# Two attentions and six layer normalisations of a decoder on one core: the softmax in row tiles, the normalisation as a pipeline over turns

## The chip, the cores and the metric

The kernel runs on one NeuronCore of one Trainium2 chip. The metric is the device time of one execution in microseconds (us), taken as the median of several executions. TensorE (PE in the profile) multiplies and transposes, VectorE (DVE), ScalarE (ACT) and GpSimd (POOL) do the rest, SyncE (SP) issues the transfers. Each engine works through its own queue in order and waits on semaphores that others raise.

## What is computed

Two decoder layers over x of 8 batches x 256 tokens x 256 features, in float32. Every sublayer is x = x + f(layernorm(x)):

```python
# layer 0: attn (causal, 16 query heads, 4 key/value heads, width 128), xattn over 64 sets, 16 experts
# layer 1: a gated delta rule (16 key heads, 32 value heads), cross attention, 48 experts
def _layernorm(x, axis=-1, eps=1e-05):
    m = jnp.mean(x, axis=axis, keepdims=True); v = jnp.var(x, axis=axis, keepdims=True)
    return (x - m) / jnp.sqrt(v + eps)
# L0 attention
scores = jnp.einsum('bkgqd,bksd->bkgqs', qg, k) * scale        # rope on q, k
attn = jax.nn.softmax(scores + causal, axis=-1)
out = jnp.einsum('bkgqs,bksd->bkgqd', attn, v)
# L1 cross attention: keys and values from 64 context rows and the 256 own rows,
# q and k first divided by their root mean square, then rope, softmax over 320 keys
```

## The kernel before, in words

The program is six blocks, one after another, with a barrier of all engines between them: self attention, set attention, routed experts, delta attention, cross attention, sparse experts. Each begins with a call of `layernorm` (L155), six in all.

**layernorm** goes over the 16 tiles of 128 tokens in four turns of four tiles. In a turn VectorE takes the statistics of four tiles (L181, L184), adds epsilon (L186); GpSimd raises to the power -1/2 (L200); VectorE scales the four tiles (L191); TensorE transposes their eight halves into banks 0 and 1 of `k.ps[0]` (L213); ScalarE copies the 128x1024 result to `xnT` (L223). VectorE has one set of statistics tiles, so turn i+1's statistics start only behind turn i's scaling, and it waits for GpSimd in each turn.

**attention** (L271) serves both attentions; `cross` tells them apart. The work is 16 units for each of two halves h (a key/value head with its G=4 query heads and one batch of 256 tokens, TB=2 row tiles). `schedule` (L346) gives every engine the same list of stages: in stage(h, front, back) the half h projects and rotates its new unit (front), while the other half g does scores, softmax, mixing and the output projection of its unit (back). Of 33 stages 31 have both; most run inside a hardware loop. The four query heads r of the back unit are done in two pairs, 0 and 1 in the first half of the stage, 2 and 3 in the second.

The queues within a stage, which set the order around the change:

- TensorE (L477): score 0, 1; project_q (L405, in cross attention one of its two tiles stands before the scores); turn_probs 0, 1 (L455); mix 0, 1 (L465); score 2, 3 (L441); project_kv (L413); turn_probs 2, 3; mix 2, 3; turn_qk (L425, L428) and give (L473), give first in cross attention.
- VectorE (L620): row_max 0, 1 (L583, L589), norm_probs 0, 1 (reciprocal L597, scaling L600), keep_probs 0, 1 (L609, L611), rotate of the two query tiles (L535 to L537), row_max 2, 3, norm_probs 2, rotate of keys, norm_probs 3, keep_probs 2, 3, in cross attention rms (L563 to L566), add_halves (L553), rms_keys (L571, L575), add_out (L617).
- ScalarE (L696): exps 0, 1 (L679), keep_probs 0, 1 (L686, L689), keep_mix 0, 1 (L694), exps 2, 3, keep_probs 2, then keep_v (L661 to L666; it waits for `rotated`, raised by the rotation of the keys), keep_probs 3, keep_mix 2, 3, keep_qk (L670, L671).
- GpSimd: the power of the sums of squares (L379, cross attention alone), the copies of tokens (L371, L373).

A semaphore of a head counts once for both row tiles: `scored`, `max_ready`, `exp_done`, `probs_ready`. mix of head r waits for both parts of keep_probs(r), ScalarE's and VectorE's.

## Time and profile before

| | us |
|---|---|
| median of 3 runs | 4150.28 (4146.95 to 4150.4) |
| the profiled execution | 4138.86 |
| its span | 4137.1 |
| TensorE busy | 3579.5, 87% |
| VectorE busy | 2639.7, 64% |
| ScalarE busy | 1644.6, 40% |
| GpSimd busy | 1412.7, 34% |

Self attention fills about 26 to 675 us of the span, cross attention about 2944 to 3870 us, delta attention about 1150 to 2889 us. The busy shares are means over blocks with different limits, so the stages of the two attentions are to be read one instruction at a time. The clock in the profile is the granted TensorE clock, 1.00 for 2.4 GHz and 0.50 for 1.2 GHz. The profiled execution is 11.4 us (0.3%) shorter than the median of the runs.

### The profile page before, as it was taken

The numbers are of one execution on the slowest core, as the hardware profiler recorded it, in microseconds if no ns is written. First come the engines' busy times: TensorE is split into PE (matmuls) and PEld (weight loads), VectorE is DVE, ScalarE is ACT, GpSimd is POOL, SyncE is SP. The second block draws the span as 40 slices with busy tenths as digits, with TensorE's granted clock in tenths as the row PEclk, the third lists the DMA queues.
The fourth block names the chain that finished last, engine by engine and source line by source line (L and its number), as shares of the span: only waits on it lengthen the run. The fifth ranks groups of instructions, "written<-read, shape, count | busy, mean of one in ns | idle before, by whom it ended". The sixth has DMA issues, their size and how long they took to land. (4 is left out here: it accounts for less than half of the span.)

```text
span 4137.1 us, 57933 instructions
## 1 busy us (share of the span) xinstructions
PE 3579.5 (87%) x17616; PEld 2756.4 (67%) x17616; DVE 2639.7 (64%) x7558; ACT 1644.6 (40%) x4218; POOL 1412.7 (34%) x2085
## 2 busy tenths in 40 slices
PE   7999997589678999999999999998499999999565
PEld 5676765445366888888888888886356556556454
DVE  5666565532247888888888888873666666666531
ACT  3444442133234455555554545441243443443221
POOL 0000000068615555555555555552111111111055
PEclk9999998589868999999999999999699999999665
DMA  2000002335500111111111111110100000000346
GB/s 75 0 0 0 0 0 68 116 65 85 117 14 19 40 28 40 29 36 30 35 37 27 37 27 39 28 21 12 57 1 0 0 0 0 0 0 0 115 111 144
DMA packets 220951, 149.99 MB, mean 36 GB/s; under 512 B 117104, under 2 KB 208656, under 8 KB 220208
## 3 DMA queue, kind: packets, MB, share of 16 engines
q1 hardware_dynamic: 193664, 111.49, 10.5%
q0 software_dynamic: 22848, 31.69, 4.6%
q10 hardware_dynamic: 4224, 4.19, 0.3%
q8 instruction: 104, 1.70, 0.2%
q14 instruction: 111, 0.91, 0.1%
HBM read 105.64 MB, written 41.61 MB: 36 GB/s over the span
## 5 line engine op out<-in xcount | busy, mean ns | idle before, releaser
L1921 DVE SCALAR_TENSOR_TENSOR dl_y<-ps,dl_taps,dl_y 128x255 f32<-128x255 f32 (+2 forms) x1536 | 652.4, 474 | 129.5 <-ACT dl_y L1817 125.3
L1652 PE MATMUL ps<-xnT,dl_wkqv 128*128 128x256 f32 x2048 | 546.2, 393 | 27.5 <-DVE dl_lp L1964 21.8
L1652 PEld LDWEIGHTS ps<-xnT,dl_wkqv 128*128 128x128 f32 x2048 | 370.7, 194 | 78.3 <-issue 34.9
L379 POOL TENSOR_TENSOR at_rs<-at_ss,mhalf 128x15 f32<-128x15 f32 x32 | 125.5, 3922 | 745.1 <-DVE at_ss L566 745.1
L1575 POOL TENSOR_TENSOR dl_rn<-dl_n,mhalf 128x4 f32<-128x4 f32 x128 | 173.4, 1354 | 548.0 <-DVE dl_n L1937 548.0
L465 PE MATMUL ps<-at_shared,at_v 128*128 128x256 f32 (+2 forms) x1280 | 315.7, 380 | 4.6
L1817 ACT ACTIVATE dl_y<-ps,dl_taps 128x256 f32<-128x256 f32 x512 | 260.2, 560 | 106.1 <-PE ps L1652 106.0
L405 PE MATMUL ps<-at_wq,at_xb 128*128 (+1 forms) x512 | 247.6, 618 | 36.0 <-POOL at_xb L373 33.9
L441 PE MATMUL ps<-at_kT,at_qT 128*128 128x320 f32 (+2 forms) x1024 | 271.2, 397 | 2.8 <-ACT at_kT L671 2.8
L1593 POOL TENSOR_TENSOR dl_inv_u<-dl_inv_u,dl_inv_tmp 64x30 f32<-64x30 f32 (+14 forms) x480 | 260.1, 542 | 37.6
L465 PEld LDWEIGHTS ps<-at_shared,at_v 128*128 128x128 f32 (+1 forms) x1280 | 211.1, 190 | 89.3 <-issue 64.0
L455 PE MATMUL ps<-ident,at_probs 128*128 128x128 f32 (+1 forms) x1152 | 173.8, 283 | 96.2 <-DVE at_probs L600 93.0
L473 PE MATMUL ps<-at_wo,at_oT 128*128 (+1 forms) x1024 | 234.8, 382 | 18.7 <-ACT at_oT L694 18.7
L1677 PE MATMUL ps<-dl_wo,dl_z 128*128 128x256 f32 x1024 | 245.9, 384 | 1.3 <-issue 1.3
L1590 POOL TENSOR_TENSOR dl_inv_tmp<-dl_inv_u,dl_inv_a 64x30 f32<-64x30 f32 (+14 forms) x480 | 233.5, 486 | 24.7
L455 PEld LDWEIGHTS ps<-ident,at_probs 128*128 128x128 f32 (+1 forms) x1152 | 124.1, 135 | 169.2 <-DVE at_probs L600 156.1
L1825 ACT ACTIVATE dl_z<-dl_y 128x512 f32<-128x512 f32 x256 | 161.6, 631 | 180.9 <-DVE dl_y L1921 180.9
L371 POOL COPY at_xb<-xnT 128x512 f32 (+1 forms) x64 | 39.1, 612 | 567.6 <-PE ps L413 562.8
L1663 PE MATMUL ps<-dl_z 128*128 128x512 f32 (+1 forms) x512 | 227.6, 528 | 0.0
L473 PEld LDWEIGHTS ps<-at_wo,at_oT 128*128 128x128 f32 x1024 | 189.4, 190 | 54.7 <-issue 27.5
L441 PEld LDWEIGHTS ps<-at_kT,at_qT 128*128 128x128 f32 x1024 | 175.3, 191 | 70.4 <-ACT at_kT L671 13.5
L583 DVE TENSOR_REDUCE at_mx<-ps 128x2 f32<-128x640 f32 x128 | 105.5, 825 | 180.5 <-PE ps L441 176.9
(348 smaller groups left out, 7798.5 us busy)
## 6 DMA issues: line engine op xcount, KB each, us to landing
dl_grow<-decay_rows SPq DMA_DIRECT2D x128, 128.0 KB, 3.0
sp_wgu<-in_w1gu SPq DMA_DIRECT2D x12, 768.0 KB, 5.3
dl_wkqv<-in_w1kqv SPq DMA_DIRECT2D x16, 512.0 KB, 4.6
delta_diag<-dl_lp SPq DMA_DIRECT2D x512, 8.0 KB
dl_diag<-delta_diag_tt SPq DMA_DIRECT2D x512, 8.0 KB, 1.7
moe_wgu<-in_w0gu SPq DMA_DIRECT2D x16, 448.0 KB, 10.6
sp_wd<-in_w1d SPq DMA_DIRECT2D x12, 384.0 KB, 6.2
dl_wo<-in_w1o SPq DMA_DIRECT2D x16, 256.0 KB, 3.6
```

The lines of the kernel that those rows point to most:

```text
L405: last = nc.tensor.matmul(k.ps[h][:, t, :], xb[h][:, c, t * P:(t + 1) * P], wq[:, c, ds(group(u) * (G * HD), G * HD)], start=c == 0, stop= ...
L441: last = nc.tensor.matmul(o[:, 0:nk], qT[h][:, r, t * P:(t + 1) * P], kT[h][:, 0:nk], start=True, stop=cross)
L455: last = nc.tensor.transpose(slot(h, (r % 2) * 4 + pieces[j])[0:w, t * P:(t + 1) * P], probs[h][:, (r % 2) * TB + t, j * P:j * P + w], k.i ...
L465: last = nc.tensor.matmul(slot(h, (r % 2) * 4 + 3)[:, c0:S], v[h][0:w, j, :], pT[h][0:w, r % 2, j, c0:S], start=j == 0, stop=j == KT - 1)
L473: last = nc.tensor.matmul(slot(h, t), oT[h][:, hh, t * P:(t + 1) * P], wo[:, ds(group(u) * G + hh, 1), :], start=hh == 0, stop=hh == G - 1)
L1590: nc.gpsimd.tensor_tensor(tmp, inv_u[:, 0:i, i:i + 1].to_broadcast([GP, i, w]), inv_a[:, i:i + 1, i + 1:Q32].to_broadcast([GP, i, w]), ALU ...
L1593: nc.gpsimd.tensor_tensor(inv_u[:, 0:i, i + 1:Q32], inv_u[:, 0:i, i + 1:Q32], tmp, ALU.subtract)\
L1652: last = nc.tensor.matmul(bank(h, m // 2, (m % 2) * S, (m % 2 + 1) * S), wkqv[h][:, c, m * P:(m + 1) * P], k.xnT[:, c, u.seq * S:(u.seq + ...
L1663: last = nc.tensor.matmul(bank(h, blk, 0, 2 * (S - blk * P)).rearrange("p (a s) -> p a s", a=2), z[h][:, 0, blk * P:(blk + 1) * P], z[h][: ...
L1677: last = nc.tensor.matmul(bank(h, 3, t * D, (t + 1) * D), z[h][:, 2 + m, t * P:(t + 1) * P], wo[h][:, m, :], start=m == 0, stop=m == 1)
L1817: last = nc.scalar.activation(y[h][:, m, :], bank(h, m // 2, (m % 2) * S, (m % 2 + 1) * S), ACT.Identity, bias=taps[h][:, m, KC:KC + 1], s ...
L1921: last = nc.vector.scalar_tensor_tensor(y[h][:, m, back:S], bank(h, m // 2, (m % 2) * S, (m % 2 + 1) * S - back), taps[h][:, m, KC - 1 - b ...
```

## The change

1. `layernorm` keeps two sets of statistics tiles. VectorE takes turn i+1's statistics before it scales turn i. It scales two of the four tiles; ScalarE scales the other two with an Identity activation whose scale is the inverse deviation and whose bias is minus mean times it, which VectorE computes in one small instruction (`ln_nmr`). Turns alternate between banks 0, 1 and 2, 3, and ScalarE's copy of turn i comes behind its scaling of turn i+1.
2. The softmax of both attentions goes by row tile: the four semaphores count each tile. The VectorE order of a pair of heads is max r t0, max r t1, max r+1 t0, norm r t0, max r+1 t1, norm r t1, norm r+1 t0, keep_probs r, norm r+1 t1, in the function `softmax`.
3. The rotation of the keys stands behind the whole `softmax` of heads 2 and 3 instead of between their scalings.
4. GpSimd's power is split into one element of the context keys and the 10 columns of the two token tiles (before: 15 columns at once, with a memset of ones ahead of the loop, now gone).

```diff
@@ layernorm, VectorE
-            for i in range(turns):
+            def stats(i):
...
+                if n >= 2:
+                    dve.wait_ge(k.ln_normed_d, n - 1)
...
+            def normalise(i):
+                n, b = i + base, i % 2
+                if n >= 1:
+                    dve.wait_ge(k.ln_normed_a, n)
+                    dve.wait_ge(k.ln_turned_d, n)
+                dve.wait_ge(k.ln_pow, n + 1)
+                nc.vector.scalar_tensor_tensor(k.ln_nmr[b][:, HQ:Q], k.ln_mv[b][:, HQ:Q, 0], -1.0, k.ln_rstd[b][:, HQ:Q],
+                                               ALU.mult, ALU.mult).then_inc(k.ln_shift, 1)
+                for q in range(HQ):
...
+            stats(0)
+            for i in range(turns):
+                if i + 1 < turns:
+                    stats(i + 1)
+                normalise(i)
@@ layernorm, TensorE (and the same for the other two tiles behind ln_normed_a)
+                n, b = i + base, 2 * (i % 2)
+                if n >= 2:
+                    pe.wait_ge(k.ln_stored, n - 1)
+                pe.wait_ge(k.ln_normed_d, n + 1)
@@ layernorm, ScalarE
             for i in range(turns):
-                act.wait_ge(k.ln_turned, i + base + 2)
-                nc.scalar.copy(k.xnT[:, :, i * Q * P:(i + 1) * Q * P], k.ps[0][:, 0:DC, :]).then_inc(k.ln_stored, 1)
+                n, b = i + base, i % 2
+                if n >= 1:
+                    act.wait_ge(k.ln_turned_a, n)
...
+                act.wait_ge(k.ln_shift, n + 1)
+                for q in range(HQ, Q):
+                    last = nc.scalar.activation(xn(i, q), k.x[:, i * Q + q, :], ACT.Identity,
+                                                bias=k.ln_nmr[b][:, q:q + 1], scale=k.ln_rstd[b][:, q:q + 1])
+                last.then_inc(k.ln_normed_a, 1)
+                if i >= 1:
+                    keep(i - 1)
+            keep(turns - 1)
@@ attention, GpSimd
-                    nc.gpsimd.tensor_tensor(rs[h][:, :, :], ss[h][:, :, :],
-                                            k.mhalf[:, 0:KT * (G + 1)].rearrange("p (t g) -> p t g", t=KT), ALU.pow)\
+                    nc.gpsimd.tensor_tensor(rs[h][0:CTX, TB, G:G + 1], ss[h][0:CTX, TB, G:G + 1], k.mhalf[0:CTX, 0:1], ALU.pow)
+                    nc.gpsimd.tensor_tensor(rs[h][:, 0:TB, :], ss[h][:, 0:TB, :],
+                                            k.mhalf[:, 0:TB * (G + 1)].rearrange("p (t g) -> p t g", t=TB), ALU.pow)\
                         .then_inc(s.rms_ready[h], 1)
@@ attention, TensorE: score raises scored once a tile; turn_probs
-                    pe.wait_ge(s.probs_ready[h], u * G + (r + 1))
+                    pe.wait_ge(s.probs_ready[h], u * (G * TB) + (r * TB + 1))
+                    for j in range(2 if cross else 1):
+                        turn(j, 0)
+                    pe.wait_ge(s.probs_ready[h], u * (G * TB) + (r * TB + 2))
+                    for j in range(2):
+                        last = turn(j, 1)
+                    if cross:
                         for t in range(TB):
+                            last = turn(2, t)
@@ attention, VectorE
+                def softmax(h, u, r):
+                    row_max(h, u, r, 0)
+                    row_max(h, u, r, 1)
+                    row_max(h, u, r + 1, 0)
+                    norm_probs(h, u, r, 0)
+                    row_max(h, u, r + 1, 1)
+                    norm_probs(h, u, r, 1)
+                    norm_probs(h, u, r + 1, 0)
+                    keep_probs(h, u, r)
+                    norm_probs(h, u, r + 1, 1)
@@ stage, VectorE
                     if back is not None:
-                        row_max(g, back, 0)
-                        row_max(g, back, 1)
-                        norm_probs(g, back, 0)
-                        norm_probs(g, back, 1)
-                        keep_probs(g, back, 0)
+                        softmax(g, back, 0)
                         keep_probs(g, back, 1)
                     if front is not None:
                         rotate(h, front, 0)
                         rotate(h, front, 1)
                     if back is not None:
-                        row_max(g, back, 2)
-                        row_max(g, back, 3)
-                        norm_probs(g, back, 2)
+                        softmax(g, back, 2)
                     if front is not None:
                         rotate(h, front, TB)
                     if back is not None:
-                        norm_probs(g, back, 3)
-                        keep_probs(g, back, 2)
                         keep_probs(g, back, 3)
@@ exps, ScalarE
-                    act.wait_ge(s.max_ready[h], u * G + (r + 1))
                     for t in range(TB):
+                        act.wait_ge(s.max_ready[h], u * (G * TB) + (r * TB + t + 1))
...
-                    last.then_inc(s.exp_done[h], 1)
+                        last.then_inc(s.exp_done[h], 1)
```

row_max(h, u, r, t) is one reduction of one tile (128, 256 or 320 columns), a wait for it, and the small instruction that forms the exp's bias; norm_probs(h, u, r, t) is one reciprocal, a wait for it, and one scaling.

## Rows read from the trace of the kernel before

**Rows 1.** Busy time by stretch (PE, PEld, DVE, ACT, POOL, clock, DMA): self and cross attention.
```profile
300.00:400.00 100.00, 92.16 (x480) 69.90 (x478) 61.54 (x196) 40.03 (x135) 3.08 (x5) 1.00 0.00 0
...
3300.00:3400.00 100.00, 92.12 (x399) 61.02 (x400) 60.79 (x162) 40.62 (x106) 17.43 (x12) 1.00 0.00 0
```
**Rows 2.** Timeline of TensorE, self attention: start, length, line, idle before it and releaser.
```profile
313.13 0.55 PE L455 MATMUL ps<-ident,at_probs 128*128 128x128 f32 x3 [0.92 <-DVE at_probs L600]
...
315.46 1.09 PE L425 MATMUL ps<-ident,at_t 128*128 128x128 f32 x8 [0.40 <-DVE at_t L553]
```
**Rows 3.** Timeline of VectorE in the same stage.
```profile
304.21 0.55 DVE L600 TENSOR_SCALAR at_probs<-at_probs,at_rden 128x128 f32<-128x128 f32 x2
306.01 0.62 DVE L611 COPY at_shared<-ps 128x128 f32<-128x128 f32 x2 [1.26 <-PE ps L455]
306.55 0.68 DVE L535 TENSOR_TENSOR at_t<-ps,rope_cos 128x512 f32<-128x512 f32 x1
...
309.07 0.61 DVE L589 TENSOR_REDUCE at_mx<-ps 128x1 f32<-128x128 f32 x2
...
309.82 0.62 DVE L589 TENSOR_REDUCE at_mx<-ps 128x1 f32<-128x128 f32 x2
...
310.87 0.17 DVE L597 RECIPROCAL at_rden<-at_den 128x2 f32<-128x2 f32 x1 [0.22 <-ACT at_probs L679]
...
313.72 0.29 DVE L611 COPY at_shared<-ps 128x128 f32<-128x128 f32 x1 [0.44 <-PE ps L455]
313.92 1.48 DVE L553 TENSOR_TENSOR at_t<-at_t 128x1280 f32<-128x1280 f32 x1
```
**Rows 4.** Timeline of TensorE, one cross-attention stage.
```profile
3312.88 0.87 PE L455 MATMUL ps<-ident,at_probs 128*128 128x128 f32 x6 [0.26 <-DVE at_probs L600]
3313.59 3.34 PE L465 MATMUL ps<-at_shared,at_v 128*128 128x256 f32 x12
...
3323.55 0.87 PE L455 MATMUL ps<-ident,at_probs 128*128 128x128 f32 x6 [1.10 <-DVE at_probs L600]
```
**Rows 5.** Timeline of VectorE in the same stage.
```profile
3312.74 0.41 DVE L609 COPY at_shared<-ps 64x256 f32<-64x256 f32 x1
...
3318.24 0.82 DVE L583 TENSOR_REDUCE at_mx<-ps 128x2 f32<-128x640 f32 x1 [1.52 <-PE ps L441]
...
3322.50 0.21 DVE L537 TENSOR_TENSOR at_t<-ps,rope_sc 64x64 f32<-64x64 f32 x1
```
**Rows 6.** Timeline of ScalarE in the same stage.
```profile
3322.97 1.03 ACT L661 ACTIVATE at_shared<-ps 128x1024 f32<-128x1024 f32 x1
...
3324.72 0.61 ACT L686 COPY at_shared<-ps 128x512 f32<-128x512 f32 x1
...
3327.64 0.37 ACT L694 COPY at_oT<-ps 128x256 f32<-128x256 f32 x1 [1.31 <-PE ps L465]
```
**Rows 7.** Timeline of all engines, second layernorm: first turn and last copy.
```profile
676.19 1.41 DVE L181 BATCH_NORM_STATS2 ln_stats<-x 128x6 f32<-128x256 f32 x4 [0.89 <-PEq L99]
...
679.42 1.38 DVE L191 TENSOR_SCALAR ln_xn<-x,ln_mv,ln_rstd 128x256 f32<-128x256 f32 x4 [1.20 <-POOL ln_rstd L200]
...
680.86 1.97 PE L213 MATMUL ps<-ident,ln_xn 128*128 128x128 f32 x8 [6.28 <-DVE ln_xn L191]
...
696.38 1.01 ACT L223 COPY xnT<-ps 128x1024 f32<-128x1024 f32 x1 [3.49 <-PE ps L213]
```
**Rows 8.** Busy time by stretch, columns as in rows 1, end of the first layernorm.
```profile
24.00:26.00 2.00, 1.09 (x6) 0.69 (x4) 0.00 (x0) 0.87 (x1) 0.00 (x0) 1.00 0.00 0
```
**Rows 9.** Timeline of TensorE: the first projection of self attention.
```profile
27.20 6.33 PE L405 MATMUL ps<-at_wq,at_xb 128*128 128x512 f32 x8 [2.10 <-POOL at_xb L371]
```
**Rows 10.** Groups by line and shape: count | busy us, mean ns | idle before.
```profile
L600 DVE TENSOR_SCALAR at_probs<-at_probs,at_rden 128x320 f32<-128x320 f32 x256 | 87.3, 383 | 4.5
...
L379 POOL TENSOR_TENSOR at_rs<-at_ss,mhalf 128x15 f32<-128x15 f32 x32 | 125.5, 3922 | 745.1 <-DVE at_ss L566 745.1
...
L1817 ACT ACTIVATE dl_y<-ps,dl_taps 128x256 f32<-128x256 f32 x512 | 260.2, 560 | 106.1 <-PE ps L1652 106.0
```

More of the change, by code:

```diff
@@ L158, in layernorm @@
     nc = k.nc
-    Q = LN_TILES
+    Q, HQ = LN_TILES, LN_TILES // 2
     turns = NT // Q
@@ L387, in stage @@
                             invert_rms(h, front)
-                if cross:
-                    for h in range(2):
-                        nc.gpsimd.memset(ss[h][:, :, :], 1.0)
                 schedule(pool, stage)
@@ L594, in norm_probs @@
[L594 to L602 removed]
+                        ins_ = nc.vector.scalar_tensor_tensor(nb[h][:, m:m + 1], mx[h][:, m:m + 1], -1.0,
+                                                              esc[h][:, t, r:r + 1], ALU.mult, ALU.mult)
+                    else:
+                        ins_ = nc.vector.tensor_scalar(nb[h][:, m:m + 1], mx[h][:, m:m + 1], -scale, None, ALU.mult)
```

107 lines of the change are left out of this document (57 added, 50 removed).

## The prediction

> **What bounds the kernel now.** I read the busy time by stretch first. In both attentions TensorE is busy 92% of the time at a granted clock of 1.00 (2.4 GHz), VectorE 61 to 62%, ScalarE 40% [rows 1]. The gaps are on TensorE, so I read its timeline through one stage of each attention. A self-attention stage has two: 0.92 us before the turning of head 3 waits for VectorE's scaling, and 0.40 us before turn_qk for VectorE's add_halves [rows 2]. A cross-attention stage has 0.26 us in its first half and 1.10 us in its second for the same scalings [rows 4], a further 0.43 us before head 2's turning and some 0.6 us before the output projection. A mean of 61% hides that VectorE has long idle time near a stage's end and next to none in the middle: in the self stage from 306.01 to 315.40 it idles 0.22 and 0.44 us between long runs of work [rows 3]. So a stage is bound by TensorE at its ends and by VectorE in its middle, and what VectorE gets to do in the middle is paid at once. The layernorms stand alone between barriers and are bound by a chain through VectorE, GpSimd, VectorE again, TensorE and ScalarE [rows 7]. All sums below are against the profiled execution, 4138.9 us; the median of the runs is 4150.3, so 11.4 us go on top at the end.
>
> **Layernorm.** Before: from the first statistics at 676.19 to the end of the last copy at 697.39, 21.2 us for four turns [rows 7]. After, VectorE's work in a turn is four statistics (1.41, with the wait behind them 1.44), their aggregation and epsilon (0.50), the new small instruction (0.08) and two scalings of 0.33, together 2.7 us, and GpSimd's power lies beside the next statistics. ScalarE scales two tiles: the nearest row is an activation with scale and bias from memory, 0.56 us for 256 columns [rows 10], two of them overlapping 1.03, and its copy 1.01: 2.0 a turn. TensorE's eight transposes take 1.97 [rows 7]. I follow the chain from 676.19: statistics of turns 0 and 1 are done at 680.1, normalise(0), (1), (2) begin at 680.1, 682.8, 685.4 (VectorE bound), normalise(3) must wait until turn 2's first two tiles are turned, 687.5; ScalarE's share of turn 3 waits for all of turn 2 (688.3) and ends at 689.35, TensorE ends at 690.5, the copy at 691.55. Gain 5.8 us a call. In five calls nothing else holds the next block. In the first the weights do: transfers end about 24 us (none left from 24 to 26 us [rows 8]) and the first projection starts at 27.20 [rows 9], so the gain there is 2.8, not 5.8. Sum: 5 x 5.84 + 2.8 = **32.0 us less**. Bounds: if ScalarE's two scalings cost 0.3 us more a turn, 28; if the tail does not wait, 36.
>
> **Self attention, first half of a stage.** VectorE is early here: both heads are scaled at 304.76, then it idles 1.26 us until TensorE, through with project_q, has turned head 0 [rows 3]. After the change the queue says: copy of head 0, then the scaling of head 1's second tile. So work that used the idle time is now queued behind a wait that ends only at 306.01. From there: copy 0.20 (start to start), reciprocal 0.20 (0.17 [rows 3] and its wait), scaling of 256 columns 0.36, to TensorE 0.06, its two remaining transposes 0.40, back 0.04, copy of head 1 0.20: the rotation starts at 307.47 instead of 306.55 [rows 3]: **+0.92**. Who waits for it: TensorE's turning and mixing of both heads, and all of VectorE's second half.
>
> **Second half.** A pair of maxima in one head cost 0.75 us from start to start (309.07 to 309.82 [rows 3]). Split, it is 0.31 + 0.11 + 0.44 + 0.11 = 0.97, since the two reductions no longer overlap and there is a second small instruction: +0.22, twice. A second reciprocal per head: +0.20, twice. Together +0.84 on VectorE between the rotation of q and add_halves. Against it stand its waits in this stretch, 0.28 behind the maxima (0.22 marked) and 0.53 for head 3's turning (0.44 marked) [rows 3], which this work fills; a new one of 0.14, where the copy of head 2 waits for its turning, comes in, and rounding of the starts adds 0.05. The second half costs +0.2. Rotating the keys behind the softmax makes ScalarE's keep_v and, queued behind it, keep_probs 3 late by 1.5 us, but mix 3 still ends 0.2 before add_halves. So add_halves ends at 316.5 instead of 315.4, turn_qk follows, and behind it TensorE's order to the next stage is unchanged: **+1.1 us a stage**. The TensorE wait of 0.92 is not gained; it is spread over three others.
>
> **Cross attention.** First half: copy of head 0 still starts at 3312.65 to 3312.74 [rows 5], takes 0.34, reciprocal 0.20, scaling 0.38 [rows 10], to TensorE 0.06, then four transposes of 0.12 (six before the mixing took 0.71 [rows 4]): mixing starts at 3314.11 instead of 3313.59, +0.52, although 0.26 of waiting goes. Second half, shifted by 0.52: the first maximum no longer waits for both tiles, 0.54 us less, so it starts at 3318.22, as before at 3318.24 [rows 5]. A tile's maximum and its small instruction take 0.62 (0.82 for two tiles [rows 5]; one I put at 0.48), reciprocal and scaling 0.50. Four maxima and three scalings: 3322.21; the copy of head 2 waits for TensorE to 3322.58, 0.34; last scaling 0.50: 3323.42; only now the rotation of keys, 1.27, so `rotated` comes at 3324.69 instead of 3322.71 [rows 5]. ScalarE's keep_v can't start at 3322.97 [rows 6] but at 3324.73; keep_probs 3, queued behind it, starts 1.76 later than 3324.72 [rows 6] and ends at 3327.09. Head 3's mixing waits for that; before it started at about 3325.9 without waiting. With half of 3.34 us [rows 4] it ends at 3328.78; ScalarE's copy of it moves from 3327.64 [rows 6] by 1.18, and the output projection with it. What VectorE does for rms and the keys comes 1.4 later, and GpSimd's power, 3.92 for 15 columns [rows 10], becomes shorter by some 1 us if it goes by columns; both stay under the 3.7 us of the output projection. If the power stayed at 3.92, turn_qk would be late by 0.2 more. The old wait of up to 0.1 at turn_qk goes. **+1.15 us a stage.**
>
> **The sum.** 31 stages have both a front and a back: 31 x 1.1 + 31 x 1.15 = 69.8 us more; the stages at the ends I put at nothing (one half alone has no rotation to delay, and the finer tiles and the added instructions cancel within 0.1 us). 69.8 - 32.0 = +37.8: 4176.7 against the profiled 4138.9, **4188 us** against the median of 4150.3. Bounds of the stage cost: 0.7 (links between instructions free, TensorE's share shorter by one transpose) and 1.6 us (each of the 16 added waits a stage costs 0.03 in a loop), with the layernorm's 28 to 36: from +8 to +71, 4158 to 4221.
>
> The Trainium skill (VectorE: DVE Perf Modes, "The DRAIN you can't avoid") says that a semaphore after each VectorE operation costs nothing extra against one after the last. The rows speak against that here: the two reductions of 128 and 256 columns end 0.61 us after the first starts [rows 3] and would take 0.75 with a wait in between. By the page the self stage would lose 0.24 us of its cost, 7 us in all.
>
> **Rivals.** (1) *The finer tiles close the gaps.* TensorE's waits for scalings, 0.92 in a self stage and 0.26 + 0.43 + 1.10 in a cross stage [rows 2, 4], go and nothing takes their place: 31 x 2.7 = 84 us less, with the layernorm 116: 4034 us. It decides where the last scaling of a pair ends before TensorE asks. For it: exps overlap with maxima of the next tile. Against it: the 1.26 us of idle time is TensorE's lateness [rows 3], and the new queue puts a scaling behind it. The Trainium skill (Perfetto Trace Analysis, "Optimizing Scalar/DVE Operations") holds this rule: where these engines aren't saturated but cause bubbles on others, breaking instructions up may let work complete sooner. (2) *The attentions stay as long as they are*: what the order costs is what the tiles bring. It needs 1.1 us of gain a stage, as when the first turned piece could be copied before TensorE is through with project_q. Then only the layernorms count: 4118 us, faster. (3) *VectorE becomes the bound of the middle more than I count*: 0.06 us for each added wait is 1.0 us a stage more, 62 us: 4250 us. (4) *The layernorm isn't pipelined in effect*, since each engine still waits for another's last piece: its 32 us stay, 4220 us.
>
> **How the numbers follow.** Forecast 0.66, rival 1 0.07, rival 2 0.12, rival 3 0.10, rival 4 0.05. Rivals 1 and 2 lie at 4034 and 4118, together 0.19, and are left out of the range; it takes in the forecast's 4158 to 4221, rival 4 and a part of rival 3, and on the low side some of the space between: 4140 to 4240. 0.2% of this kernel, 8 us, is what a measurement can tell from no change. Within the forecast 0.03 lies so near; with a part of the space between it and rival 2, same gets 0.05. Faster 0.17, slower 0.78.
>
> **What would show it.** Right: self stages of about 20.9 us where output additions are 19.8 apart, cross stages of 29.4 where they are 28.2; TensorE idle before the second transposes of head 1 by 0.6 to 0.9 us; in cross attention ScalarE's keep_v waiting for `rotated`, and TensorE waiting for keep_probs 3 by more than 1 us; layernorms of 15.4 us. Wrong: TensorE busy over 93% in the attentions, copies of head 0 that start before project_q ends, or layernorms still at 21.

## The result, and the profile after

The changed kernel takes **4239.36 us** (median of 6 runs, 4234.66 to 4242.42) against 4149.56 us of the kernel before (4144.17 to 4151.7): a ratio of 1.0221, 95% interval 1.0209 to 1.0233. It is slower, as forecast, but by 90 us and not by 38. Its profiled execution spans 4237.4 us; the one of before spans 4137.1, so between the two traces 100.3 us are to be explained, and it is these that the parts below add up to.

First the busy time of the same two stretches as in [rows 1] (length, then busy time and count of PE, PEld, DVE, ACT and POOL, then the granted clock, DMA share, GB/s):

```profile
300.00:400.00 100.00, 87.56 (x433) 65.41 (x432) 63.77 (x226) 38.81 (x127) 3.07 (x5) 0.97 0.00 0
3300.00:3400.00 100.00, 89.42 (x367) 59.79 (x366) 60.73 (x187) 39.78 (x101) 13.38 (x12) 0.95 0.00 0
```

TensorE's busy share fell from 92 to 88 and 89%: a stage is longer with the same work. The other number is new: the clock was 1.00 in both, and is 0.97 and 0.95 now.

The lengths of stages I read from VectorE's output additions, one for each stage: in self attention 21.0 to 21.1 us where they were 19.77, but in 8 of the 31 stages 22.4 to 22.5; in cross attention 30.6 and 30.8 in turn where they were 28.1 and 28.4. The first two cross stages took 28.97 and 29.32; they are the only two in which the clock stayed at 1.00. By blocks, from first to last addition and from layernorm to layernorm:

| stretch | before | after | difference | forecast |
|---|---|---|---|---|
| self attention | 611.3 | 661.0 | +49.7 | +34.1 |
| cross attention | 876.5 | 946.5 | +70.0 | +35.7 |
| the rest (six layernorms, and the blocks between them) | | | -19.4 | -32.0 |

**TensorE in a self stage.** The timeline at the place of [rows 2], in one of the long stages (first its first half, then its second), the clock of the same microseconds, and the transposes of turn_qk one stage later:

```profile
303.47 0.44 PE L492 MATMUL ps<-ident,at_probs 128*128 128x128 f32 x2 [0.73 <-DVE at_probs L645]
...
309.77 0.71 PE L492 MATMUL ps<-ident,at_probs 128*128 128x128 f32 x3 [0.86 <-DVE at_probs L645]
...
311.05 0.44 PE L492 MATMUL ps<-ident,at_probs 128*128 128x128 f32 x2 [0.57 <-DVE at_probs L645]
...
312.45 1.50 PE L512 MATMUL ps<-at_shared,at_v 128*128 128x256 f32 x4 [0.31 <-ACT at_shared L736]
313.75 1.91 PE L465 MATMUL ps<-ident,at_t 128*128 128x128 f32 x8
```

```profile
310.00:312.00 2.00, 1.43 (x9) 0.99 (x7) 1.82 (x9) 0.62 (x2) 0.00 (x0) 1.00 0.00 0
312.00:314.00 2.00, 1.69 (x8) 1.37 (x7) 1.32 (x1) 0.68 (x4) 0.00 (x0) 0.66 0.00 0
314.00:316.00 2.00, 2.00 (x11) 2.00 (x10) 0.00 (x0) 0.37 (x1) 0.00 (x0) 0.50 0.00 0
```

```profile
335.88 1.09 PE L465 MATMUL ps<-ident,at_t 128*128 128x128 f32 x8
```

In the first half the wait of 0.73 us is new. In the second, waits of 0.86, 0.57 and 0.31 us stand where 0.92 and 0.40 stood; behind them the clock falls to 0.50, which is 1.2 GHz, and the eight transposes of turn_qk take 1.91 us where they took 1.09 [rows 2]. One stage later the same waits (0.90, 0.56 and 0.31 us) bring no fall, and the transposes take 1.09 again: the fall comes in 8 of the first 30 stages.

**VectorE's queue, one stage later** (start, length, line; at the place of [rows 3]):

```profile
325.14 0.29 DVE L655 COPY at_shared<-ps 128x128 f32<-128x128 f32 x1 [1.51 <-PE ps L492]
...
325.54 0.35 DVE L645 TENSOR_SCALAR at_probs<-at_probs,at_rden 128x256 f32<-128x256 f32 x1
...
326.42 0.29 DVE L655 COPY at_shared<-ps 128x128 f32<-128x128 f32 x1 [0.53 <-PE ps L492]
326.63 0.68 DVE L584 TENSOR_TENSOR at_t<-ps,rope_cos 128x512 f32<-128x512 f32 x1
...
329.15 0.28 DVE L632 TENSOR_REDUCE at_mx<-ps 128x1 f32<-128x128 f32 x1
...
331.62 0.60 DVE L645 TENSOR_SCALAR at_probs<-at_probs,at_rden 128x256 f32<-128x256 f32 x1
...
334.35 1.48 DVE L602 TENSOR_TENSOR at_t<-at_t 128x1280 f32<-128x1280 f32 x1
```

From the first copy to the rotation 1.49 us (0.54 before, 1.46 forecast), from the first maximum to add_halves 5.20 (4.85 before, 5.07 forecast).

**A cross stage**, TensorE and below it the clock:

```profile
3310.92 0.66 PE L492 MATMUL ps<-ident,at_probs 128*128 128x128 f32 x4 [0.78 <-DVE at_probs L645]
...
3320.78 0.66 PE L492 MATMUL ps<-ident,at_probs 128*128 128x128 f32 x4 [0.75 <-DVE at_probs L645]
...
3324.35 1.76 PE L512 MATMUL ps<-at_shared,at_v 128*128 128x256 f32 x6 [1.42 <-ACT at_shared L733]
...
3326.67 5.36 PE L520 MATMUL ps<-at_wo,at_oT 128*128 x16 [0.56 <-ACT at_oT L741]
```

```profile
3324.00:3326.00 2.00, 1.65 (x6) 0.97 (x6) 1.97 (x5) 0.57 (x2) 0.57 (x1) 1.00 0.00 0
3326.00:3328.00 2.00, 1.44 (x4) 1.16 (x4) 0.96 (x2) 0.37 (x1) 2.00 (x2) 0.65 0.00 0
3328.00:3330.00 2.00, 2.00 (x6) 1.55 (x6) 0.87 (x3) 0.00 (x0) 1.89 (x3) 0.50 0.00 0
3330.00:3332.00 2.00, 2.00 (x12) 1.72 (x11) 0.36 (x2) 0.00 (x0) 0.00 (x0) 0.99 0.00 0
```

And the same place in the kernel before, with turn_qk behind it:

```profile
3328.16 3.71 PE L473 MATMUL ps<-at_wo,at_oT 128*128 x16 [0.56 <-ACT at_oT L694]
3332.04 1.09 PE L425 MATMUL ps<-ident,at_t 128*128 128x128 f32 x8 [0.16 <-DVE at_t L575]
```

The forecast waits are there: 0.78 for the scaling behind the copy, and 1.42 for ScalarE's copy of head 3's turned piece (called its third copy below). Behind them comes what was not forecast: the output projection of 16 matmuls takes 5.36 us where it took 3.71, because the clock granted is 0.50 for some 3 us. In the kernel before the same stretch had 1.00 throughout.

**A layernorm** (start, length, engine and line; [rows 7] has the same one before): first statistics and last copy, then the first matmuls of the block behind it, in the changed kernel and in the kernel before.

```profile
723.91 1.41 DVE L186 BATCH_NORM_STATS2 ln_stats<-x 128x6 f32<-128x256 f32 x4 [0.89 <-PEq L99]
...
738.75 1.01 ACT L251 COPY xnT<-ps 128x1024 f32<-128x1024 f32 x1 [0.31 <-PE ps L242]
...
740.07 6.69 PE L844 MATMUL ps<-xnT,set_wq 128*128 128x256 f32 x16 [1.35 <-PEq L172]
```

```profile
697.70 5.60 PE L797 MATMUL ps<-xnT,set_wq 128*128 128x256 f32 x16 [1.35 <-PEq L168]
```

15.85 us instead of 21.20, and the block behind it begins with a loss of 1.09 us: its first 16 matmuls take 6.69 us instead of 5.60, at a mean granted clock of 0.55 instead of 0.65.

### The profile page after: what moved, and what is told of

Same layout as the page of the kernel before. It is cut to its first block and busy times, and to the rows that moved or that the text cites. A ratio compares the mean times of both kernels' runs of the same rounds, so it can differ in the third digit from the quotient of the medians.

```text
span 4237.4 us, 60483 instructions
## 1 busy us (share of the span) xinstructions
PE 3636.4 (86%) x17616; PEld 2795.6 (66%) x17616; DVE 2700.5 (64%) x8174; ACT 1687.0 (40%) x4266; POOL 1404.9 (33%) x2115
## 5 line engine op out<-in xcount | busy, mean ns | idle before, releaser
L512 PE MATMUL ps<-at_shared,at_v 128*128 128x256 f32 (+2 forms) x1280 | 328.6, 385 | 53.6 <-ACT at_shared L733 43.9
L422 POOL TENSOR_TENSOR at_rs<-at_ss,mhalf 64x1 f32<-64x1 f32 x32 | 55.3, 1730 | 825.2 <-DVE at_ss L615 825.2
L632 DVE TENSOR_REDUCE at_mx<-ps 128x1 f32<-128x320 f32 (+2 forms) x512 | 215.8, 422 | 138.8 <-PE ps L481 131.4
L520 PE MATMUL ps<-at_wo,at_oT 128*128 (+1 forms) x1024 | 282.3, 437 | 18.7 <-ACT at_oT L741 18.7
L492 PE MATMUL ps<-ident,at_probs 128*128 128x128 f32 (+1 forms) x1152 | 192.1, 286 | 123.1 <-DVE at_probs L645 123.1
L520 PEld LDWEIGHTS ps<-at_wo,at_oT 128*128 128x128 f32 x1024 | 224.0, 225 | 67.8 <-issue 27.5
```

The lines of the kernel that those rows point to most:

```text
L492: return nc.tensor.transpose(slot(h, (r % 2) * 4 + pieces[j])[0:w, t * P:(t + 1) * P], probs[h][:, (r % 2) * TB + t, j * P:j * P + w], k.i ...
L512: last = nc.tensor.matmul(slot(h, (r % 2) * 4 + 3)[:, c0:S], v[h][0:w, j, :], pT[h][0:w, r % 2, j, c0:S], start=j == 0, stop=j == KT - 1)
L520: last = nc.tensor.matmul(slot(h, t), oT[h][:, hh, t * P:(t + 1) * P], wo[:, ds(group(u) * G + hh, 1), :], start=hh == 0, stop=hh == G - 1)
```

## The experiments

Two theories stood at the start. **The theory:** two orders in VectorE's queue lengthen a stage (the copy of the first head's turned piece ahead of the second's last scaling, and in cross attention the keys' rotation behind the whole softmax), and the longer waits of TensorE bring the clock down, which costs as much again. **The rival:** the split itself costs, by its second reciprocals, small instructions and waits. Each ratio is to runs of the kernel before on the same chip.

### The copy behind the last scaling

```diff
                     norm_probs(h, u, r + 1, 0)
-                    keep_probs(h, u, r)
                     norm_probs(h, u, r + 1, 1)
+                    keep_probs(h, u, r)
```

> The changed kernel with one order taken back: VectorE's copy of the first head's turned piece stands behind the second head's last scaling, not before it. Theory (the queue order, and the granted clock behind it): in cross attention the last scaling of head 1 and of head 3 no longer waits behind a copy, so TensorE's waits of 0.78 and 0.75 us go, the keys' rotation comes 1.5 us earlier, the wait of 1.42 for ScalarE's third copy shrinks to nothing, and with less waiting the clock stays at 1.00 in the output projection (3.7 instead of 5.4 us): a stage of about 28.0 instead of 30.7. In self attention 20.1 to 20.3 instead of 21.0, and no stage of 22.4. Together about 110 to 125 us less: 4115 to 4130. If the clock falls for a reason that has nothing to do with these waits: stages of 29.3 and 20.2, every third still 1.4 longer: 4165 to 4175. Rival (the split itself costs: two reductions that no longer overlap, second reciprocals, waits of each tile): the order is worth at most 0.3 us a stage, 4220 to 4239.

Measured: ratio 1.0052 (1.0036 to 1.0069), 4165.12 us. Self stages are 19.77 and 19.82 us, none longer: the self attention takes 611.2 us, what it took before the change. So in self attention the order of this one copy was the whole loss, falls of the clock included, and all the added reciprocals, small instructions and waits cost nothing that can be seen. The rival falls there. In cross attention the first seven stages take 30.9 to 31.2 us, and from then on they go 27.9, 30.0, 30.8, 28.1, 29.7, 31.0 us in turn. The short ones are what I expected; my expectation that the wait for ScalarE's third copy would go was wrong, and with it the total of 4115 to 4130. The time lies where I had put a clock that falls regardless of these waits (4165 to 4175), but not for that reason: the self stages have no fall left. TensorE in such a stage, then the clock one stage later:

```profile
3302.76 1.76 PE L512 MATMUL ps<-at_shared,at_v 128*128 128x256 f32 x6 [1.75 <-ACT at_shared L733]
3305.13 3.71 PE L520 MATMUL ps<-at_wo,at_oT 128*128 x16 [0.61 <-ACT at_oT L741]
```

```profile
3330.00:3333.00 3.00, 1.76 (x6) 0.97 (x6) 2.90 (x5) 1.42 (x6) 0.92 (x1) 1.00 0.00 0
3333.00:3336.00 3.00, 2.69 (x6) 2.19 (x7) 0.83 (x3) 0.16 (x1) 3.00 (x3) 0.54 0.00 0
```

Counted from the stage's first score, TensorE reached that wait 1.4 us earlier than in the changed kernel, and ScalarE's copy came 1.1 us earlier, so the wait is 1.75 us long instead of 1.42. The clock falls in 22 of the first 30 stages.

### Work for TensorE in the waits

```diff
+                def fill(h, m, count):
+                    for _ in range(count):
+                        nc.tensor.transpose(slot(h, m)[:, 0:P], k.ident[:, :], k.ident[:, :])
                 def mix(h, u, r):
+                    if cross and r == 3:
+                        fill(h, 0, 10)
                     pe.wait_ge(s.probs_kept_a[h], u * G + (r + 1))
...
                 def give(h, u):
+                    if cross:
+                        fill(h, 0, 4)
```

> The changed kernel with work added to TensorE and nothing taken away: in cross attention, in front of the wait for head 3's third copy, ten transposes of the identity into a bank that nobody uses then, and four more in front of the wait before the output projection. They end before the waits do (1.42 and 0.56 us; a transpose takes 0.11 to 0.12), so by themselves they gain nothing. Theory (the clock falls because TensorE waits there): the granted clock stays at 1.00 in cross attention, the output projection takes 3.7 instead of 5.36 us, a stage 29.3 instead of 30.72, 45 us less in all: about 4194. Rival (the clock has another cause, or the longer output projection hides something just as late): 4239 or a little more, stages of 30.7, with the clock still at 0.5 between 23 and 26 us after the stage's first score.

Measured: ratio 1.0161 (1.0144 to 1.0177), 4206.35 us. Nothing was taken away and TensorE has 14 transposes more in each cross stage, and the stage fell from 30.7 to 29.32 us (29.17 and 29.46 in turn, no fall in the first 30), 908.6 instead of 946.5 us in all. The traces differ by 38 us; by the ratios, 1.0221 and 1.0161, the gain is about 25 us, with some 8 either way (the profiled execution is the shortest of four, and I had expected 45). Its TensorE, and the clock:

```profile
3309.92 1.31 PE L508 MATMUL ps<-ident 128*128 128x128 f32 x10
3311.41 1.76 PE L518 MATMUL ps<-at_shared,at_v 128*128 128x256 f32 x6 [0.18 <-ACT at_shared L741]
3313.09 0.66 PE L508 MATMUL ps<-ident 128*128 128x128 f32 x4
3313.72 3.71 PE L528 MATMUL ps<-at_wo,at_oT 128*128 x16
```

```profile
3314.00:3316.00 2.00, 2.00 (x11) 1.74 (x11) 0.01 (x1) 0.00 (x0) 2.00 (x2) 1.00 0.00 0
```

The projection is back at 3.71 us. This separates the two parts of the cross stage's loss: 29.32 - 28.24 = 1.08 us are the queue's order (forecast 1.15), 1.4 are the clock (forecast nothing). The changed kernel's own first two stages, 28.97 and 29.32 without a fall, say the same. Self attention, where no work was added, kept its 8 long stages.

### The layernorm alone

The kernel before with the new `layernorm` and its tiles, both attentions untouched; the diff of the layernorm is the one shown with the change.

> The kernel before with the new layernorm alone, attentions untouched. By the prediction 32.0 us less than before: 4118. By the trace of the changed kernel a layernorm takes 15.85 instead of 21.20 us (5.35 less), and the five that nothing else holds give 26.8, the first 2.0: 4121. But in that trace the stretches between the attentions were only 12.9 shorter and the one behind them 4.5, since the blocks after a layernorm start at half the clock for longer: 4149.6 - 2.0 - 12.9 - 4.5 = 4130. Rival (nothing gained where the layernorm stands, since its successor waits for its weights): 4145 to 4150.

Measured: ratio 0.9942 (0.9925 to 0.9958), 4117.57 us against 4141.29. That is 24 us less (17 to 31); 32 lies just outside. Its attentions are those of before (self 19.77, cross 28.23). The first projection starts at 24.33 us instead of 27.20 [rows 9], 2.87 earlier, where the prediction had 2.8, and it waits for the weights:

```profile
24.33 5.62 PE L448 MATMUL ps<-at_wq,at_xb 128*128 128x512 f32 x8 [4.85 <-DMA at_wo<-in_w0o]
...
688.20 6.47 PE L840 MATMUL ps<-xnT,set_wq 128*128 128x256 f32 x16 [1.35 <-PEq L172]
```

The second of these rows is the block behind the second layernorm: 6.47 us, as long as in the changed kernel.

### Work for TensorE beside the layernorm

```diff
+            fill(14)
             for i in range(turns):
                 n, b = i + base, 2 * (i % 2)
                 if n >= 2:
                     pe.wait_ge(k.ln_stored, n - 1)
+                if i > 0:
+                    fill(4)
...
                 last.then_inc(k.ln_turned_a, 1)
+            fill(14)
```

(`fill` is as above, into the other half of the PSUM; the rest is the layernorm alone.)

> The kernel before with the new layernorm, and in each layernorm transposes of the identity on TensorE into a bank that is not used there: 14 ahead of the first turn, 4 in front of each further turn's wait, 14 behind the last. Theory (what the layernorms' gain lacks against 32 us is the clock of 0.5 at which they and the first matmuls behind them run): the real transposes take 0.6 instead of 1.09 us a half, the block behind the first of the two mixtures starts at full clock (16 matmuls in 5.6 instead of 6.7 us): 4 to 12 us less than the layernorm alone, a ratio to before of 0.991 to 0.993. Rival (the layernorm is bound by VectorE, and what follows waits for other things): no difference to the layernorm alone, 0.994, or more, where the added transposes delay the real ones.

Measured: ratio 0.9909 (0.9894 to 0.9924), 4102.73 us against 4137.89. The intervals of 0.9942 and 0.9909 just fail to overlap, on two chips; that the added transposes gain something is likely and not beyond doubt. The trace shows what they do:

```profile
686.17 0.66 PE L249 MATMUL ps<-ident,ln_xn 128*128 128x128 f32 x4
686.66 1.69 PE L231 MATMUL ps<-ident 128*128 128x128 f32 x14
688.65 3.69 PE L848 MATMUL ps<-xnT,set_wq 128*128 128x256 f32 x16 [0.30 <-PEq L172]
```

In the last two turns the real transposes of half a turn take 0.66 instead of 1.06 us, and the next block's first 16 matmuls 3.69 instead of 6.47. From the first statistics to the next block's first matmul it is 15.3 us instead of 16.1: the layernorm becomes only a little shorter, since VectorE bounds most of it, as forecast. In the two traces the six layernorms are 0.9 to 1.2 us shorter each, and the block behind the second is 2.0 us shorter.

### The keys' rotation early

```diff
                     norm_probs(h, u, r, 1)
+                    if between is not None:
+                        between()
                     norm_probs(h, u, r + 1, 0)
...
-                        softmax(g, back, 2)
-                    if front is not None:
-                        rotate(h, front, TB)
+                        softmax(g, back, 2, None if front is None else lambda: rotate(h, front, TB))
+                    else:
                         rotate(h, front, TB)
```

> The changed kernel with the other order taken back: VectorE rotates the keys ahead of head 3's first scaling, as early as before, not behind the whole softmax. Theory: in cross attention the square of the projections starts 1.2 us earlier and the wait of 1.42 for ScalarE's third copy goes, but head 3's scalings come 1.27 later and TensorE waits for them 2.0 instead of 0.75: the stage changes by -0.3 to +0.2 us, the clock falls as often. In self attention the rotation (0.7 us) goes the same way: 0 to +0.3. In all 4225 to 4250. Rival (the late rotation is what costs in the second half and what lets the clock fall): stages of 29.3 or less in cross attention, 4190 or below.

Measured: ratio 1.0121 (1.0104 to 1.0138), 4191.61 us. My theory was wrong here and the rival right: cross stages are 28.51 and 28.80 us, with one fall of the clock in the first 30, although TensorE waits longer for head 3's scaling:

```profile
3314.88 0.44 PE L492 MATMUL ps<-ident,at_probs 128*128 128x128 f32 x2 [1.14 <-DVE at_probs L645]
3315.70 0.66 PE L492 MATMUL ps<-ident,at_probs 128*128 128x128 f32 x4 [0.38 <-DVE at_probs L645]
3316.19 3.34 PE L512 MATMUL ps<-at_shared,at_v 128*128 128x256 f32 x12
3320.10 3.72 PE L520 MATMUL ps<-at_wo,at_oT 128*128 x16 [0.56 <-ACT at_oT L743]
```

The waits of 1.14 and 0.38 take the place of 0.75 and 1.42; I had added the rotation's whole 1.27 to the 0.75. Then both mixes run without a pause. Apart from the clock, the late rotation cost 29.32 - 28.65 = 0.7 us of the cross stage. In self attention the same order costs 0.4 us more, and the clock falls in 12 stages instead of 8.

### The copy's order in one half alone

```diff
+                    if r == 0:
+                        norm_probs(h, u, r + 1, 1)
+                        keep_probs(h, u, r)
+                        return
                     keep_probs(h, u, r)
                     norm_probs(h, u, r + 1, 1)
```

> The changed kernel with the copy's order taken back in the first half of a stage alone (heads 0 and 1). By the prediction's terms the first half carries 0.92 of the 1.25 us that this order costs in self attention and 0.52 of the 1.3 in cross attention: self stages of about 20.1 instead of 21.02, cross stages (clock apart) 0.5 less than now. With the stages in which the clock falls: self none or few of them, cross as many as now; 31 x 0.92 + 8 x 1.4 + 31 x 0.52 = 56 us less: ratio to before about 1.009. Rival (both halves cost alike, since each has the same queue): 0.65 in both, self stages 20.4, ratio 1.010 to 1.013.

and the same with `r == 2`:

> The changed kernel with the copy's order taken back in the second half of a stage alone (heads 2 and 3). By the prediction's terms what is left of the order's cost: self stages of about 20.7 instead of 21.02, cross stages 0.8 less than now (clock apart), with the clock falling as often as now: 31 x 0.3 + 31 x 0.8 = 34 us less: ratio to before about 1.014. Rival (both halves alike): self stages of 20.4, ratio 1.010 to 1.013.

Measured: the first half alone 1.0035 (1.0021 to 1.005), the second alone 1.0206 (1.0189 to 1.0223). I had written 1.009 and 1.014, so the first half is worth more and the second less than the prediction's terms; the rival, both alike, is wrong by more.

| us a stage | changed | first half back | second half back | both back |
|---|---|---|---|---|
| self, without a fall | 21.04 | 19.86 | 20.81 | 19.79 |
| self, stages with a fall | 8 | 0 | 5 | 0 |
| cross, without a fall, two in turn | 29.2, 29.5 (with the added transposes) | 28.2, 28.5 | 28.6, 28.8 | 27.9, 28.1 |
| cross, mean of the first 30 stages | 30.62 | 29.46 | 30.75 | 29.86 |

The first half carries 1.18 us in self attention and about 1.0 in cross (forecast 0.92 and 0.52); 0.96 of the 1.18 lie between the first copy and the rotation, the rest is a shift against GpSimd, below. The last column but one is the lesson: with the second half taken back a cross stage without a fall is 0.6 us shorter, and the mean is not, because the clock takes more of it. TensorE there:

```profile
3325.38 0.66 PE L492 MATMUL ps<-ident,at_probs 128*128 128x128 f32 x4 [0.78 <-DVE at_probs L645]
...
3338.45 2.12 PE L512 MATMUL ps<-at_shared,at_v 128*128 128x256 f32 x6 [1.75 <-ACT at_shared L737]
```

Even the mixing behind the wait is slow there, 2.12 instead of 1.76 us. What was won on VectorE became TensorE's wait of 1.75 where 1.42 had been, and the clock took it.

### The kernel before, made late

```diff
+                def wait_a_while(h, u):
+                    for i in range(6):
+                        nc.scalar.copy(late[h][:, :], k.ident[:, :]).then_inc(lated[h], 1)
+                        act.wait_ge(lated[h], u * 6 + (i + 1))
...
                         keep_v(h, front)
+                        if cross:
+                            wait_a_while(h, front)
```

> The kernel before, nothing of the change in it, with one lateness added in cross attention: behind ScalarE's keep_v six small copies one after the other (about 0.3 us each, 1.8 in all), so that its copy of head 3's turned piece comes so much later; mix 3 has 0.6 us of slack there, so TensorE gets a wait of about 1.2 us that it had not. Theory (the clock falls because TensorE waits in several places of a stage, whatever makes it wait): the output projection behind that wait runs partly at half the clock, 5.4 us instead of 3.7, and a stage takes 28.24 + 1.2 + 1.4 = 30.8: 80 us more than before, about 4222. Rival (the lateness costs what it is, and the fall belongs to something else in the change): 29.4 a stage with the clock at 1.00, 37 us more, about 4180.

Measured: ratio 1.0179 (1.0163 to 1.0195), 4213.94 us. Nothing of the change is in this kernel, and a wait of 1.44 us before mix 3 brings the fall: the mean of the first 30 cross stages is 30.74. The mean is what I wrote, the pattern is not: 12 of them take 29.3 to 29.5 without a fall, 9 take about 30.8, and 9 about 32.5, so a fall costs 1.4 or 3.2 us, and not every stage has one. One of the long ones:

```profile
3327.25 2.06 PE L467 MATMUL ps<-at_shared,at_v 128*128 128x256 f32 x6 [1.44 <-ACT at_shared L693]
3329.92 6.40 PE L475 MATMUL ps<-at_wo,at_oT 128*128 x16 [0.61 <-ACT at_oT L701]
```

With the transposes that removed the fall, this shows the cause from both sides: a wait put into the kernel before brings it, work in the waits of the changed kernel takes it away.

### The order and the waits together

The copy behind the last scaling, and the same 10 and 4 transposes in cross attention:

> The changed kernel with the copy's order taken back, as before, and in cross attention ten transposes of the identity in front of the wait of 1.75 us for head 3's third copy and four in front of the wait of 0.61 before the output projection. Without them the cross stages went in a pattern of 27.9, 30.0, 30.8, 28.1, 29.7, 31.0. Theory (the slow ones are the clock alone): all stages 27.9 to 28.2, 1.7 us less on average: 52 us less than 4165, about 4113. Rival (a stage alternates for another reason, such as the queue's state): the mean stays near 29.6 and the time near 4165.

Measured: ratio 0.9923 (0.9908 to 0.9939), 4108.92 us: cross stages of 28.09 and 28.37 in turn (one of the first is 28.58), the clock 1.00 in all of them. The unevenness of the copy's order alone was the clock alone. The stage itself is now that of before (28.24), with the layernorm's gain beside it.

### Both orders taken back, and with the layernorm's transposes

In cross attention the rotation goes ahead of head 3's first scaling, in self attention it stays behind the softmax; the copy is behind the last scaling in both:

```diff
-                        softmax(g, back, 2)
-                    if front is not None:
+                        softmax(g, back, 2, (lambda: rotate(h, front, TB)) if cross and front is not None else None)
+                    if front is not None and not (cross and back is not None):
                         rotate(h, front, TB)
```

> The changed kernel with both orders taken back where each costs: the copy of the first head's turned piece behind the second head's last scaling in both attentions, and in cross attention alone the rotation of the keys ahead of head 3's first scaling. Theory: self stages 19.8 without a fall of the clock; cross stages without the wait of 1.75 that the copy's order alone left, so the clock stays up: 28.65 (rotation alone taken back) less the 0.78 of the first half and up to 0.38 in the second: 27.5 to 27.9, and the new layernorm on top: 4090 to 4108, faster than the layernorm alone (24 us under before). Rival (the clock falls in some stages as with the copy's order alone): cross stages of 29 to 30, 4135 to 4165.

Measured: ratio 0.9883 (0.9867 to 0.9899), 4089.62 us against 4137.89. Cross stages are 27.48 and 27.76, self stages 19.8, the clock 1.00 in both attentions. This kernel is faster than the changed one and the one before, and faster than the layernorm alone: once the queue lets it, the change brings 0.62 us in a cross stage. Its trace shows where, read against the kernel before:

```profile
3293.26 3.72 PE L520 MATMUL ps<-at_wo,at_oT 128*128 x16 [0.56 <-ACT at_oT L743]
3296.88 1.09 PE L465 MATMUL ps<-ident,at_t 128*128 128x128 f32 x8
...
3315.99 1.15 PE L492 MATMUL ps<-ident,at_probs 128*128 128x128 f32 x6 [1.14 <-DVE at_probs L645]
```

```profile
3291.90 1.73 POOL L422 TENSOR_TENSOR at_rs<-at_ss,mhalf 64x1 f32<-64x1 f32 x1 [23.15 <-DVE at_ss L615]
3293.60 1.96 POOL L423 TENSOR_TENSOR at_rs<-at_ss,mhalf 128x10 f32<-128x10 f32 x1
```

From a stage's first score to the first mixing it is 6.23 us instead of 6.53 (the wait of 0.26 [rows 4] is gone), from there to the output projection 14.53 instead of 14.60: these 0.37 us can be the finer tiles. The other 0.25 are not: from the output projection to turn_qk it is 3.60 us instead of 3.85, on average over 26 stages, and GpSimd's power, which turn_qk needs by way of VectorE, ends 2.28 instead of 2.53 us behind the projection's start. That goes with the split of the power. It is read from the traces alone: no run has the finer tiles without the split. With the transposes beside the layernorms on top:

> The new layernorm with the transposes of the identity beside it, the softmax by row tiles with the copy behind the last scaling in both attentions, and in cross attention the rotation of the keys ahead of head 3's first scaling. Theory (the two gains lie in different blocks and add): ratio to before 0.9883 - 0.0033 = 0.985, about 4076, self stages 19.8, cross stages 27.6, clock 1.00 in both. Rival (the transposes gave nothing, and the layernorm alone with and without them differed by the chips): 0.988.

Measured: ratio 0.9867 (0.9851 to 0.9884), 4089.1 us against 4142.35. The fastest of all, but the step from 0.9883 lies within the intervals: that the transposes add here is open, and the 0.985 that I had written lies just outside. In the two traces the last five layernorms are 1.2 us shorter each, but delta attention, the same code in both, took 7.7 us longer.

## Why the prediction was right or wrong

**The direction, and its reason: right.** An order in VectorE's queue puts a scaling behind a copy that must wait for TensorE, and the stage pays. The self stage grew by 1.27 us (forecast 1.1), the cross stage, clock apart, by 1.08 (1.15). From the traces: self attention +49.7 less 11.2 for the eight long stages is 38.5; cross attention +70.0 less the 37.9 that the filled waits gave back is 32.1; together **70.6, where the sum had 69.8**. That the totals agree so closely is luck in part: self attention cost 4.4 us more than its term and cross attention 3.6 less.

**Self attention, first half: right.** From the first copy to the rotation 1.49 us against the 1.46 that the steps gave; with the order taken back 0.53.

**Self attention, second half: nearly right.** 5.20 against 5.07 us. Forecast as nothing and found: the scaling of 256 columns takes 0.60 us at 331.62 while GpSimd copies tokens, 0.35 elsewhere. With the first half taken back, GpSimd's copy starts later than this scaling, it takes 0.35, and the stretch is 4.95 us long: that is the 0.2 us of that experiment beyond 0.96. The split of a pair of maxima cost what was said: 0.97 us from the first to the third maximum (329.15 to 330.12), 0.75 before. The Trainium skill (VectorE: DVE Perf Modes, "The DRAIN you can't avoid") has it that a semaphore behind each operation costs nothing extra; on VectorE the pair is 0.22 longer. The two are not quite the same thing: here a dependent instruction waits for each reduction, and a second such instruction takes 0.09 of the 0.22 (329.47 to 329.56). But with the copy behind the scaling this 0.22 is hidden, and the stage is as long as before.

**Cross attention, the queue: right in sum, wrong in shares.** Mixing starts 0.51 us later in the stage (0.52 forecast) and the output projection 1.20 (1.18), both read from the stage's first score. But 0.52 + 0.63 was written as if the first half's copy cost 0.52 only; taking back the first half alone gives 1.0 us, the second 0.6, both 1.3. The parts are not additive, since they meet in one wait, the 1.42 for ScalarE.

**"TensorE's order to the next stage is unchanged", and the output projection's 3.7 us as cover: the step that failed.** The prediction read a clock of 1.00 in [rows 1] and carried it over to a stage in which it had itself forecast new waits of 0.6 to 0.9 and of over 1 us. It had the cause in its hands and gave it no term. It costs 11.2 us in self attention (eight stages 1.4 us too long; no run filled the waits there) and 37.9 in cross (with the waits filled): **49 us, nearly the whole difference** between forecast and result in the attentions (119.7 against 69.8). The upper bound of the stage's cost, 1.6 us, was made of small waits alone, and lacked it as well; the cross stage was 2.48 us longer.

**The layernorm: mechanism right, size too large.** 15.85 us against 15.4; a gain of 5.35 a call against 5.84. The chain written down has VectorE's turns 2.7 and 2.6 us apart and the trace has 2.75 and 2.83; the two activations take 1.09, not 1.03. With 2.87 for the first that is 29.6, not 32.0. The trace with the layernorm alone is 27.0 us shorter than that of before, the changed kernel's rest 19.4. In the changed kernel five layernorms are 5.4 us shorter each and the way to the first self-attention addition 2.0 us, 29.1 together; the blocks behind them give 9.8 back. Against the kernel before they take 2.1, 2.9, 1.8, 2.1 and 1.0 us longer, though their code is the same (but for the fourth, which reaches to the first addition of cross attention and so into changed code). Of the first of these, 1.09 us are its first 16 matmuls at the low clock. With the transposes beside the layernorm that block and the next are as short as before (69.8 and 340.2 us against 70.2 and 340.8), which speaks for the clock there; for the rest the cause stays open: the stretch between the fourth and the fifth layernorm, whose code is the same in all these kernels apart from the layernorm, took 1757.4, 1752.8, 1753.0 and 1759.5 us in four of them, so that single traces differ by more than what is sought.

**The split of GpSimd's power: wrong in size.** It was put at about 1 us shorter by columns. The two parts take 1.73 us for 64x1 and 1.96 for 128x10, 3.7 together against 3.92 [rows 10]. In the changed kernel the slowed output projection hides it. With both orders taken back it does count: it is 0.25 of the 0.62 us that a cross stage gains.

**The rivals.** Rival 3 (0.06 us for each added wait, 4250) came nearest to the time, and only with a part of it does the stated range reach 4240, just beyond the measured 4239, which is luck. It is wrong: with all these waits in place and one copy moved, self attention is as long as before. A time that fits is no evidence for its mechanism. Rival 4 is wrong: the layernorm is pipelined. Rival 2 is wrong as the kernel stands. Rival 1 is wrong too, but its idea was half right: with both orders mended, cross stages are 0.6 us shorter than before (not 1.8), at most 0.4 of it by the finer tiles, self stages not at all. That is as far as the rule of the Trainium skill goes here (Perfetto Trace Analysis, "Optimizing Scalar/DVE Operations": smaller instructions may let work complete sooner); which piece stands behind which in the queue decided it.

## What to carry to other kernels

When work is cut finer, write down for each in-order engine which piece stands behind a wait that it doesn't itself need: one copy ahead of one scaling cost 50 us in self attention alone, and with both orders mended the same change brought 23 us in cross attention (876.4 to 853.6), some 8 of them by the shorter way through GpSimd, 4 in the last stage, where the clock no longer falls, and at most 11 by the finer cutting. When a forecast adds waits to the busiest matmul engine, give the clock a term of its own, with the price read from rows at either level (16 matmuls: 3.71 us and 5.36), and look at it in slices of 2 us, not of 100. And after moving work off one engine, ask which wait grows by it. Ahead of the output projection a cross stage's marked waits on TensorE came to 1.79 us before, 2.95 in the changed kernel, 1.75 with the copy back, 2.30 with the rotation back and 1.14 with both, and the stages without a fall of the clock follow: 28.2, 29.3, 28.0, 28.7 and 27.6 us.

## What the runs showed of the hardware

- The granted clock fell from 1.00 to 0.50 (2.4 to 1.2 GHz) for about 3 us behind a group of waits (0.75, 1.42 and 0.56 us), about as the last of them ended (0.65 on average from 3326 to 3328 us, 0.50 in the two behind). So the matmuls that pay are those after the waits, and the rows of the waits show nothing of it. Waits of 1.14, 0.38 and 0.56 us, with both mixes run without a pause, brought one fall in the first 30 stages.
- With waits of the same length the fall comes in some stages and not in others, and costs 1.4 or 3.2 us (stages of 29.3, 30.8 and 32.5 in the kernel made late; the low clock lasts about twice as long in the last of these).
- Transposes of the identity that nobody reads, put in waits, took the trace's cross attention from 946.5 to 908.6 us; placed beside the layernorm they took the next block's first 16 matmuls from 6.47 to 3.69 us.
- In self attention a scaling of 128x256 on VectorE that began while GpSimd copied 128x512 took 0.53 to 0.72 us (29 of them in the changed kernel), and 0.35 otherwise. In the experiment with the first half taken back it began before the copy and took 0.35, and the scaling of 128x128 behind it took 0.44 to 0.58 instead of 0.29.
- GpSimd's power took 1.73 us for one column on 64 partitions, 1.96 for ten on 128, and 3.92 for fifteen on 128: cutting it by rows and columns saved 0.2 us.
